# The gate matmuls of the context move ahead of the score turn in a two-way interleaved recurrent stage

## What is computed

```python
def step(h, x_t):
    proj = h @ W
    score = jnp.einsum('bsh,bh->bs', enc_hiddens, proj)
    attn = jax.nn.softmax(score, axis=-1)
    context = jnp.einsum('bs,bsh->bh', attn, enc_hiddens)
    inp = jnp.concatenate([x_t, context], axis=-1)
    gx = inp @ kernel + bias
    gh = h @ recurrent_kernel
    z = jax.nn.sigmoid(xz + hz)
    r = jax.nn.sigmoid(xr + hr)
    cand = jnp.tanh(xh + r * hh)
    h_new = z * h + (1.0 - z) * cand
    return (h_new, h_new)
```

## Time and profile before

| | us |
|---|---|
| three runs | 7572.54, 7583.25, 7591.73 |
| median | 7583.25 |
| the profiled execution | 7594.07 |
| its span | 7592.0 |

### The profile page before, as it was taken

The page is one execution under the profiler, slowest core; times in us unless marked ns, Lnnn a source line. Parts: engine busy times, 40 slices in busy tenths (PEclk is TensorE's granted clock), DMA queues, the critical chain, the costliest instruction groups (busy, mean ns, idle before and its releaser), DMA issues. The chain is left out here.

```text
span 7592.0 us, 189244 instructions
## 1 busy us (share of the span) xinstructions
PE 5998.1 (79%) x79720; PEld 4371.9 (58%) x79720; DVE 4815.5 (63%) x16917; ACT 2874.7 (38%) x4943; POOL 1029.5 (14%) x924
## 2 busy tenths in 40 slices
PE   4454569889878778787699688888888788888887
PEld 3343446566665567676577456556566555565655
DVE  6777964554567666666544576575675775765864
ACT  1221224444425211111112165455455454554663
POOL 1113521211200200000000111110110111011101
PEclk7667879999989655555599898999989999989999
DMA  1000000000000000000000000000000000000000
GB/s 33 1 0 3 1 29 1 1 1 1 1 5 2 6 3 3 3 3 3 24 1 1 19 2 2 11 2 2 11 2 2 11 2 7 6 2 10 2 2 15
DMA packets 61231, 44.75 MB, mean 6 GB/s; under 512 B 22521, under 2 KB 56125, under 8 KB 60227
## 3 DMA queue, kind: packets, MB, share of 16 engines
q1 hardware_dynamic: 60355, 32.26, 1.6%
HBM read 30.14 MB, written 2.10 MB: 4 GB/s over the span
## 5 line engine op out<-in xcount | busy, mean ns | idle before, releaser
L261 DVE TENSOR_REDUCE peak<-ps 128x8 f32<-128x1024 f32 (+1 forms) x832 | 817.1, 1024 | 262.1 <-PE ps L183 261.5
L303 ACT ACTIVATE e<-ps,H_lowT_c 77x1024 f32<-77x1024 f32 x384 | 405.6, 1105 | 271.1 <-PE ps L207 271.1
L303 ACT ACTIVATE e<-ps,H_lowT_s 128x1024 f32<-128x1024 f32 x384 | 407.0, 1111 | 249.6 <-PE ps L207 249.6
L221 PEld LDWEIGHTS ps<-e,H_vt 128*32 128x32 f32 (+1 forms) x12288 | 326.1, 113 | 261.2 <-ACT e L303 145.7
L221 PE MATMUL ps<-e,H_vt 128*32 128x128 f32 (+1 forms) x12288 | 442.3, 286 | 23.6 <-DVE xs L281 17.8
L2482 POOL TENSOR_TENSOR H_rstd<-H_veps,neghalf 128x4 f32<-128x4 f32 (+1 forms) x146 | 160.8, 1101 | 2132.1 <-DVE H_veps L2478 2132.1
L207 PE MATMUL ps<-H_qr,H_km 32*128 32x128 f32 (+1 forms) x12288 | 434.1, 281 | 0.0
L207 PEld LDWEIGHTS ps<-H_qr,H_km 32*128 32x128 f32 (+1 forms) x12288 | 419.3, 174 | 16.7 <-issue 3.7
L311 ACT ACTIVATE oT<-ps 128x512 f32<-128x512 f32 x416 | 248.4, 597 | 366.0 <-PE ps L221 366.0
L2176 ACT ACTIVATE F_ex<-ps,F_nm 16x77 f32<-16x77 f32 x256 | 81.5, 318 | 765.3 <-DVE F_nm L2088 765.3
L183 PE MATMUL ps<-H_km,H_qr 32*128 32x512 f32 (+1 forms) x3072 | 353.0, 527 | 0.0
(11 more groups left out here) (650 smaller groups left out, 13817.8 us busy)
## 6 DMA issues: line engine op xcount, KB each, us to landing
G_w<-in_L_ffn_w SPq DMA_DIRECT2D x16, 256.0 KB
H_f<-in_L_xcond_f_w SPq DMA_DIRECT2D x12, 256.0 KB
H_nw<-in_L_xcond_n_w SPq DMA_DIRECT2D x21, 128.0 KB, 2.1
A_cond<-in_cond SPq DMA_DIRECT2D x1, 2048.0 KB
out_x<-x_all SPq DMA_DIRECT2D x1, 2048.0 KB, 8.7
ctx_rows<-in_ctx SPq DMA_DIRECT2D x1, 1232.0 KB
D_wq<-in_L_xcond_attn_wq SPq DMA_DIRECT2D x2, 512.0 KB
D_wk<-in_L_xcond_attn_wk SPq DMA_DIRECT2D x2, 512.0 KB
```

The source lines that it names most:

```text
L221: last = nc.tensor.matmul(ps[PAD_COLS * s:PAD_COLS * (s + 1), FLAT, r * S:(r + 1) * S], vt_of(u)[0:keys, QUAD * r + s, :], e[0:keys, half, ...
L261: last = nc.vector.tensor_reduce(peak[:, HL * half:HL * (half + 1)], view, AX.X, ALU.max, negate=True)
L303: nc.scalar.activation(e[0:keys, half, :], ps[0:keys, AGAIN[half]:AGAIN[half] + 2, :].rearrange("p b t -> p (b t)"), ACT.Exp, bias=low(u) ...
```

## The change

In the loop over half steps on TensorE, `late(k - 1)` stands right behind `score(k)` instead of behind `turn_scores(k)`. No other engine's list changes.

```diff
                             for k in range(HALVES):
                                 score(k)
+                                if k > 0:
+                                    late(k - 1)
                                 of_state(k, PRODUCTS[0:2])
                                 turn_scores(k)
-                                if k > 0:
-                                    late(k - 1)
                                 of_state(k, PRODUCTS[2:3])
                                 turn_weights(k)
                                 of_state(k, PRODUCTS[3:5])
                                 attend(k)
```

## The result

| | before | changed |
|---|---|---|
| median of 4 runs, us | 7587.49 | 7641.11 |
| lowest and highest, us | 7572.54 and 7592.92 | 7633.06 and 7652.29 |
| span of the profiled execution, us | 7592.0 | 7631.2 |
| first to last load group of line 2024, us | 2540.9 to 3723.9 | 2549.2 to 3789.3 |

The ratio is 1.0075, 95% interval [1.0054, 1.0095]: slower, as forecast, but by 54 us where the text said 33. The last row is the sharper measure. From the first to the last score load the recurrent stage took 1183.0 us before and 1240.1 us now, 57.1 us more, which is 0.227 us in each of 252 half steps. The rest of the program took 6409.0 us in the one profiled execution and 6391.1 in the other, which hides part of it; over the thirteen traces of this case it took 6371 to 6430.

The account below looks back on a forecast made before the run. A chain of hand-overs between engines, not a full engine, was taken to bound the recurrent stage. 252 half steps x 0.13 us = 33 us, other terms 0, on 7583.25 gave 7616 us, 0.43% slower; range 7592 to 7645.

Parts of the forecast that it names:

- The chain, and that the turn heads it: Recurrent half step of 4.49 us: scores, sum, turn at line 2037, maximum, exponential, state; any delay of the turn delays everything behind.
- The pitch of the moved loads: On TensorE ahead of the turn: 26.7 ns per load, 0.40 us for 15 and 0.16 for six, turn 0.12 us late.
- rival A: Moved TensorE pairs run at 25.3 ns, near the skill's 25 ns; turn 0.09 us late, 23 us, 7606 us; chance 0.06.
- Does the step from bf16 loads to the fp32 turn cost anything without the gap?: On TensorE, from the bf16 loads straight into the fp32 turn: taken as 0, upper end 0.03 us, one slot.
- The matmul lag of 0.02 us: On TensorE at the turn: in a dense run matmuls trail their loads by 0.02 us, making the delay 0.14 us.
- Gate sums sooner worth 0: On VectorE: the gate sums' wait of 71.6 us goes, but F_eT's wait grows by as much; worth 0.
- room behind the turn worth 0: TensorE is free earlier behind the turn, but line 2041 waits for the exponential anyway; worth 0.
- The two moved waits cost 0: Waits for c_high and c_low, now ahead of the turn on TensorE, have fired already; cost 0, 0.15 us to spare.
- Clock unmoved: TensorE's granted clock in the recurrent stage stays at 0.50, that is 1.2 GHz.
- its own upper end for the step to fp32: On TensorE at the turn: with the step's upper end of 0.03 us the loss is 252 x 0.17 = 43 us.
- rival C: TensorE restarts at the two moved waits, or c_low comes late; turn 0.22 to 0.24 us late, 58 us, 7641; chance 0.09.

## Why the prediction was right, and where it was short

- *The chain, and that the turn heads it:* right. Every link behind line 2037 kept its length, and the stage grew by what the turn was late.
- *The pitch of the moved loads* (0.40 us for 15, 0.16 for six): right to 0.01 us for the 15, and for the six by their own starts; it gave 0.12 us of the 0.22. The rule of 25 ns, rival A, gave 7606 and was wrong for the clock of 0.50.
- *"Does the step from bf16 loads to the fp32 turn cost anything without the gap? ... I take 0, and for an upper end 0.03":* this is the step that failed. It cost 0.10 us, 252 x 0.10 = 25 us, about the whole miss (57.1 us of stage for 33). The question was the right one but asked of the wrong property. The rows it was answered from the earlier trace rows compare loads of 128 columns on both sides; the turn's load has 16. And it was put at zero since in the kernel before a gap hid it; an operation that has only been seen behind a gap has not shown its price without one. The matmul lag of 0.02 us, the other reading, did not come: load and matmul both start at 3005.82.
- *Gate sums sooner worth 0, and room behind the turn worth 0:* right under the old orders. The wait went over to F_eT, as foretold. The experiments show that it was worth 0.37 us a half step once VectorE's and ScalarE's orders took it up.
- *The two moved waits cost 0:* right: the 15 loads show no hole at either. The separate test moved the turn's wait and found it free too. *Clock unmoved:* right.

The forecast of 7616 us was 25 us short, inside the range of 7592 to 7645. That it fell inside is in part luck: the forecast with its own upper end for the step to fp32, 252 x 0.17 = 43 us, gives 7626, and only rival C (7641), whose mechanism the timeline shows false, carried the range to 7645. In a stage with four passes of 63 equal half steps a term of 0.10 us is 0.3% of the program.

## What to carry to other kernels

When work is moved into a gap, look at what stood right behind the gap: its instruction may have a start-up cost that the gap was hiding, so compare its load's shape, not only its type, with rows where it follows without a gap. When a move makes a result ready earlier and nothing gets faster, look whose queue order holds its user; here that order, changed together with the move, turned a loss of 0.7% into a gain of 0.6% (one execution), and into 1.0 and 1.3% with the nine matmuls of `of_state` behind the turn and then one wait less. And judge such a change by the start-to-start times of one half step and the length of the stage, since those settled differences of 0.06 us a half step that whole runs, scattered over tens of us, did not tell.

## What the runs showed of the hardware that was not expected

- Behind dense loads of 128 columns, a load of 16 or 64 columns started 0.10 us later than the pitch of 26.7 ns gives, in bf16 (16) as in fp32 (16 and 64); a load of 128 columns started on the pitch in either type. In bf16 this moved the result by 0.08 us and the half step by 0.09 to 0.10; in fp32 it brought no result forward.
- The load behind a narrow one comes late too: 0.17 us behind the start of the bf16 turn of 16 columns (3003.28 and 3003.11), 0.03 behind that of 128 (3004.93 and 3004.90).
- A wait on a signal that had fired cost nothing on TensorE where it was an instruction's only wait (one place tried). On VectorE a second wait on the same instruction, also fired 0.3 us before, went with 0.07 us between the release and the start (0.42 for 0.34), and the stage was 18.9 us shorter without it. Only that one place was tried; whether it holds in general stays open.
- Why the narrow load is held is not shown. That it starts 0.02 us behind the end of the record of the load ahead, in all kernels with the hold, says where it stands and not why.
